# Step sizes ahead of z in the scan layer's front part, a second bank for its first projections, and fewer state slices summed by TensorE

## What is computed

```
x = _layernorm(x + _L0_attn_ref(x, ...))        # scan layer
x = _layernorm(x + _L0_xattn_ref(x, ctx_768, ...))
x = _layernorm(x + _L0_ffn_ref(x, ...))         # 4 experts, 2 of them used
x = _layernorm(x + _L1_attn_ref(x, ...))        # attention, 16 heads
x = _layernorm(x + _L1_xattn_ref(x, ctx_768, ...))
x = _layernorm(x + _L1_ffn_ref(x, ...))         # recurrence over the batches

def _L0_attn_ref(x, ...):
    xn = layernorm(x) * ln_g + ln_b
    xh, z = jnp.split(xn @ W_in, 2, axis=-1)
    conv = conv_b + sum over k of conv_w[:, k] * (xh shifted by 3 - k)
    xc = silu(conv)
    xpj = xc @ W_xp                              # B (16), C (16), one step size
    dt = softplus(xpj[..., -1:] @ W_dt + b_dt)
    h[t] = exp(dt * A) * h[t-1] + dt * B * xc    # for each of 16 states
    y = sum over states of h * C + xc * D
    return y * silu(z) @ W_out + x
```

## Time and profile before

| | |
|---|---|
| median of 3 runs | 1427.11 us (1426.35 to 1427.77) |
| the profiled execution, device time | 1427.31 us |
| its span in the trace | 1425.5 us |
| TensorE busy | 1221.3 us (86% of the span) |
| VectorE busy | 1112.3 us (78%) |
| ScalarE busy | 785.0 us (55%) |
| mean granted TensorE clock | 0.93 |

### The profile page before, as it was taken

One profiled execution on the slowest core, in us unless ns is written; L12 is line 12 of the kernel. 1 busy time (PEld: TensorE's weight loads), 2 busy tenths in 40 slices (PEclk: granted clock), 3 DMA queues, 4 the chain that ended last, 5 costly groups with the idle time before them and its releaser, 6 DMA issues.

```text
span 1425.5 us, 16890 instructions
## 1 busy us (share of the span) xinstructions
PE 1221.3 (86%) x6016; PEld 973.1 (68%) x6016; DVE 1112.3 (78%) x1799; ACT 785.0 (55%) x1861; POOL 122.4 (9%) x151
## 2 busy tenths in 40 slices
PE   3587778989989899989999899999998998999862
PEld 2454556677767767776777677877786767868742
DVE  2799699799978988899989997899889883343116
ACT  1533445385465663766667666675576645545521
POOL 0000111010011002110110010101000100010001
PEclk8788889999999999999999999999999999999976
DMA  4610111200011002010111001100210000000301
GB/s 165 218 72 4 71 38 30 67 30 31 11 65 56 31 1 75 8 49 30 46 37 49 31 29 54 49 30 1 75 49 19 12 15 20 1 0 8 117 0 59
DMA packets 27638, 62.53 MB, mean 44 GB/s; under 512 B 2346, under 2 KB 13451, under 8 KB 26915
## 3 DMA queue, kind: packets, MB, share of 16 engines
q1 hardware_dynamic: 27554, 61.46, 12.6%
HBM read 55.42 MB, written 6.04 MB: 43 GB/s over the span
## 4 chain that ended last, share of the span: by engine, by line
DVE 43%; PE 36%; issue 9%; ACT 9%; POOL 2%; DMA 0%; DVEq 0%; SPq 0%; ACTq 0%; POOLq 0%
DVE scans L496 12%; PE bank L283 12%; DVE scans L492 7%; PE bank L1065 4%; PE bank L447 4%; DVE scans L502 4%; PE bank L1083 3%; DVE nmax L1219 3%; DVE conv L383 2%; PE bank L851 2%; PE bank L633 2%; ACT scans L470 2%; PE bank L1110 2%; PE bank L845 2%; DVE scans L500 2%
## 5 line engine op out<-in xcount | busy, mean ns | idle before, releaser
L496 DVE TENSOR_TENSOR_SCAN scans<-scans 128x1024 f32<-128x1024 f32 x128 | 292.7, 2287 | 11.2 <-ACT scans L470 9.4
L470 ACT ACTIVATE scans<-dt,a_neg 128x255 f32<-128x255 f32 x512 | 222.4, 503 | 113.3 <-DVE scans L496 112.9
L447 PE MATMUL bank<-scans,ident 128*128 128x256 f32 x704 | 201.1, 425 | 21.5 <-DVE scans L500 15.4
L447 PEld LDWEIGHTS bank<-scans,ident 128*128 128x128 f32 x704 | 143.4, 214 | 57.8 <-DVE scans L500 25.0
L492 DVE TENSOR_TENSOR scans<-conv,BC 128x1024 f32<-128x1024 f32 x128 | 155.6, 1216 | 14.3 <-PE bank L447 13.9
L1153 ACT ACTIVATE ya<-bank,nmax 128x256 f32<-128x256 f32 x256 | 107.1, 472 | 96.1 <-DVE nmax L1219 95.9
L1219 DVE TENSOR_REDUCE nmax<-bank 128x2 f32<-128x512 f32 x128 | 87.2, 682 | 67.4 <-PE bank L1065 67.0
L1083 PE MATMUL bank<-v,ya 128*128 128x65 f32 x1024 | 133.9, 276 | 6.1 <-ACT yo L1144 6.1
L1083 PEld LDWEIGHTS bank<-v,ya 128*128 128x128 f32 x1024 | 131.2, 199 | 10.4 <-issue 6.7
L502 DVE TENSOR_TENSOR scans<-scans,BC 128x1024 f32<-128x1024 f32 x80 | 97.5, 1219 | 1.0
L283 PE MATMUL bank<-xnT,w_in 128*128 128x256 f32 x256 | 73.9, 440 | 20.8 <-DVE conv L383 12.8
(11 more groups left out here) (255 smaller groups left out, 2170.9 us busy)
## 6 DMA issues: line engine op xcount, KB each, us to landing
BC<-xpj_scratch SPq DMA_DIRECT2D x32, 1024.0 KB, 5.5
xin<-in_x SPq DMA_DIRECT2D x8, 256.0 KB, 2.8
conv<-in_x SPq DMA_DIRECT2D x8, 256.0 KB, 2.8
out<-scans SPq DMA_DIRECT2D x8, 256.0 KB, 2.6
kept_x<-x SPq DMA_DIRECT2D x7, 256.0 KB, 2.0
kept_w<-wa SPq DMA_DIRECT2D x7, 256.0 KB, 2.0
BC<-kept_w SPq DMA_DIRECT2D x1, 1792.0 KB, 8.5
scans<-kept_x SPq DMA_DIRECT2D x1, 1792.0 KB, 13.2
```

Source lines behind the costliest of these rows:

```text
L447: last = pe.matmul(sums_of(c), ident[:, :], hb[u % 2][:, i, :], start=False, stop=(h == UH - 1 and i == summed(b) - 1), skip_group_check=True)
L470: ins = act.activation(dA[u % 2][:, j, 1:S], dt[b % 2][:, c, 1:S], ACT.Exp, scale=a_neg[:, c, n:n + 1])
L496: dve.tensor_tensor_scan(flat(H[:, :, :]), flat(dA[u % 2][:, :, :]), flat(H[:, :, :]), 0.0, ALU.mult, ALU.add).then_inc(s["a_scan"], 1)
```

## The change

- **Order in the front part.** The projections j = 2 and 3, their tanh and their product (z) stand behind dt on TensorE, ScalarE and VectorE, and no longer between the convolution and xc. The turn of the next batch waits for z in place of dt.
- **Two banks in batch 0.** Projection j = 1 of batch 0 goes to bank 2 (SA[1], not yet in use), so it doesn't wait for the convolution of j = 0.
- **The place of xpj.** It lies in rows of xin, no longer of xnT, because xnT is still needed for z. So x of the next batch is loaded only when the store has landed and the step size has been spread (`a_store`, `a_dtl_ps`); ScalarE's xnT no longer waits for the store.
- **Sums.** FULL_SUMS becomes SUMMED = (4, 4, 4, 2, 2, 1, 1, 1): in batches 5, 6 and 7 VectorE adds the two remaining slices as well (a new `tensor_tensor` of 256 columns, behind a wait on its own result), and TensorE adds one.
- **Waits at the start.** `skips`, wt0, kzE and kzO are VectorE pieces of W now (two pieces, both still first in its order); TensorE waits for each where it uses it.
- **All order strings are new.** 1100 letters of TensorE, 1018 of ScalarE, 885 of VectorE (883 before), 74 of GpSimd and 91 of SyncE.

```diff
-FULL_SUMS = 3
+SUMMED = (4, 4, 4, 2, 2, 1, 1, 1)
...
     "sp": (
-        "FWFFSSWWWSWWSFFSSSSFFSSSSSSFFSSSWSWWWSSFFSSWWWWSSFFSSSWWWWSSFFSSSWWWWSSFSSWSWWWSSWSWWWWWWWW"
+        "FWFSSWWWFSWWSFFSSSSFFSSSSSSFFSSSWSWWWSFFSSSWSWWWFFSSSSFFWSWWWSSSSWWWWSFSWSSSWWWSSWSWWWWWWWW"
...
-        xpj = xnT[0:2 * NS + 1, 0, :]
+        xpj = xin[0:2 * NS + 1, 0, :]
...
         def front_sp(sp, b):
             if b:
-                sp.wait_ge(*of("a_xnT_ps", b - 1))
+                sp.wait_ge(*of("a_store", b - 1))
+                sp.wait_ge(*of("a_dtl_ps", b - 1))
...
+        def conv_bank(b, j):
+            return SA[1] if b == 0 and j == 1 else f0
...
             if b:
-                pe.wait_ge(*of("a_dt", b - 1))
+                pe.wait_ge(*of("a_silu_z", b - 1))
             turn(pe, xin, f0).then_inc(s["a_xnT_ps"], 1)
...
-            for j in range(4):
-                if 1 <= j <= 2:
-                    pe.wait_ge(*of("a_conv", b, 2 * j))
-                elif j == 3:
-                    pe.wait_ge(*of("a_silu_z", b, 1))
...
+            for j in range(2):
+                if j and b:
+                    pe.wait_ge(*of("a_conv", b, 2 * j))
+                projected(j, conv_bank(b, j))
                 yield
             pe.wait_ge(*of("a_xc", b))
-            pe.wait_ge(*of("a_silu_z", b))
             mm(pe, f0[0:2 * NS + 1, 0:S], [(w_xp[:, c, :], xc[:, c, :]) for c in range(EC)]).then_inc(s["a_xpj_ps"], 1)
...
+            pe.wait_ge(*of("a_dt", b))
+            for j in range(2, 4):
+                if j == 3:
+                    pe.wait_ge(*of("a_silu_z", b, 1))
+                projected(j, f0)
+                yield
...
         def summed(b):
-            return HN if b < FULL_SUMS else HN // 2
+            return SUMMED[b]
...
-                    dve.tensor_tensor(flat(H[:, 0:HN // 2, :]), flat(H[:, 0:HN // 2, :]), flat(H[:, HN // 2:HN, :]), ALU.add).then_inc(s["a_hC"], 1)
+                    last = dve.tensor_tensor(flat(H[:, 0:2, :]), flat(H[:, 0:2, :]), flat(H[:, 2:4, :]), ALU.add)
+                    if summed(b) == 1:
+                        own.link(last)
+                        last = dve.tensor_tensor(H[:, 0, :], H[:, 0, :], H[:, 1, :], ALU.add)
+                    last.then_inc(s["a_hC"], 1)
...
-            pe.wait_ge(s["prep_zero"], 3 + EC)
```

More of the change, by code:

```diff
@@ L304, in front_sp @@
             yield
+        SA = bank[1:3]
+        def conv_bank(b, j):
+            return SA[1] if b == 0 and j == 1 else f0
         def front_pe(pe, b):
@@ L371, in front_act @@
             yield
+            for j in range(2):
+                act.wait_ge(*of("a_in_ps", b, j + 3))
+                act.activation(flat(zg[b % 2][:, 2 * j:2 * j + 2, :]), f0[:, :], ACT.Tanh).then_inc(s["a_z_tanh"], 1)
+                yield
         def front_dve(dve, own, b):
@@ L405, in front_dve @@
             yield
+            for j in range(2):
+                z = flat(zg[b % 2][:, 2 * j:2 * j + 2, :])
+                dve.wait_ge(*of("a_z_tanh", b, j + 1))
+                dve.scalar_tensor_tensor(z, z, 1.0, f0[:, :], ALU.add, ALU.mult).then_inc(s["a_silu_z"], 1)
+                yield
         def front_pool(pool, own, b):
@@ L410, in front_pool @@
             yield
-        SA = bank[1:3]
         def sums_of(c):
@@ L1054, in y_pe @@
             yield
+            if b == 0:
+                pe.wait_ge(s["prep_zero"], 3)
             pe.wait_ge(*of("t_kz", b))
@@ L1313, in halves, with zeros @@
             dve.wait_ge(s["prep_halves"], 3)
+        def zeros(dve):
+            for c in range(EC):
+                dve.tensor_scalar(skips[:, c, :], ident[:, :], d_skip[:, c:c + 1], None, ALU.mult).then_inc(s["prep_skips"], 1)
+            dve.memset(wt0[CTX2:P, 1, :], 0.0).then_inc(s["prep_zero"], 1)
+            yield
+            dve.memset(kzE[HD:P, :, :], 0.0).then_inc(s["prep_zero"], 1)
+            dve.memset(kzO[0:HD, :, :], 0.0).then_inc(s["prep_zero"], 1)
+            yield
         def p_dve(dve, own):
+            yield from zeros(dve)
             dve.wait_ge(s["prep_pe"], 1)
```

87 lines of the change are left out of this document (38 added, 49 removed).

## The result

The changed kernel takes **1444.62 us** (median of 4 runs, 1442.38 to 1445.34) beside 1426.76 us for the kernel before in the same series: a ratio of 1.0119, 95% interval 1.0106 to 1.0132. It is 17 us slower by that ratio (18.0 in the profiled spans, 1443.5 beside 1425.5). The prediction was 1417 us, faster, with a range of 1398 to 1431: wrong in sign and outside its range.

A forecast was written before the change was run, and what follows sets the result against it. No engine alone bounds the kernel: VectorE early, both nearly full in batches 5 to 7, TensorE at the end. Terms -10.0 + 2.5 - 1.1 - 6.3 + 9.5 - 5.0 = -10.4 us: 1417 us, range 1398 to 1431.

The forecast's parts named there:

- The head: Front part of batch 0: a shorter chain starts the first unit at 46.0 instead of 56.04 us, gain 10.0 us.
- The bound of 7 us: Lower bound of the head's gain (bounds 7 and 13), expected if the skill's clock rule alone held.
- Batch 0's scan: First stage: +2.5 us of VectorE work, -1.1 us of waiting for dt; batch 0's residual 8.6 us earlier.
- Batches 1 to 4: Pieces put off, weighed by chain shares: 6.3 us earlier by batch 4's end; ends 9.7 and none.
- Batches 5 to 7: Additions and returning put-off pieces, weighed by chain shares: 9.5 us later; ends 26.6 later and 5.3 earlier.
- VectorE's idle time stays: Outer end for batches 5 to 7: VectorE's idle time does not fall, so 26.6 us come in.
- Behind the last scan: After batch 7's scan: fewer Y and W pieces left on TensorE, 5 us earlier.
- VectorE decides in batches 5 to 7: Rival: additions between scan and sum, VectorE's idle time unchanged, 26.6 us come in: 1434 us, chance 0.12.
- TensorE decides: Rival: from 154 us on, time follows TensorE's work, -27.7 us in all: 1399 us, chance 0.17.
- The clock: Rival: TensorE's clock falls by 0.02 over 425 us of work, costing some 8 us: 1425; 0.15 with the lost start.
- the 0.96 that I had named as a sign: Stages of batches 5 to 7: a clock under 0.96 was to show the forecast wrong.
- The early start lost: Rival: the first stage ends no earlier than before, 8.6 us go: 1425 us; chance 0.15 together with the clock.

The follow-up runs named there:

- e15: Changed kernel without the 48 additions of batches 5 to 7, TensorE still summing one slice a unit there: 1428.32 us, ratio 1.0012 to the kernel before.
- e6: Changed order up to batch 0's first units, z behind dt in batch 0 only, then the old order, no additions: 1425.56 us, 0.9994 of the kernel before.
- e12: e6 with TensorE's sum of the first unit moved ahead of the transposition of batch 1's x: 1421.85 us, ratio 0.9966 to the kernel before.
- e3: Changed kernel up to the end of batch 4's scan, then the old order, two slices, no additions: 1423.8 us, ratio 0.9991 to the kernel before.
- e14: Kernel before, TensorE summing one slice a unit in batches 5 to 7, no additions on VectorE: 1422.08 us, ratio 0.9969 to the kernel before.
- e2: Kernel before with only the changed sums (additions on VectorE, one slice on TensorE in batches 5 to 7): 1440.04 us, ratio 1.0098.
- e1: Changed kernel without the additions of batches 5 to 7, TensorE summing two slices, new order throughout: 1443.94 us, ratio 1.0124 to the kernel before.
- e4: Changed kernel up to the end of batch 4's scan, then the old order, with the additions: 1441.56 us, ratio 1.011 to the kernel before.
- e9: Changed kernel, TensorE summing only 16 of 256 columns of the remaining slice in batches 5 to 7: 1444.19 us, ratio 1.0122 to the kernel before.
- e13: Changed kernel with the additions kept, but TensorE summing two slices a unit in batches 5 to 7: 1447.24 us, ratio 1.0142 to the kernel before.

## Why the prediction was wrong

**The head: right.** Predicted 46.0 for the first unit, measured 45.80 (44.0 to 45.8 in the twelve profiles that begin with this order); xpj was ready at 35.8 (35.3). The bound of 7 us, which I had drawn from the Trainium skill's rule (page "TensorE: Matmul & The Clock Gate", section "HAM oscillation — how this bites in real kernels": bursts with idle gaps between run throttled), was not reached: skips and w_xp both ran slow, which cost 1 us more than I took, but the 16 preparation matmuls ran fast again, in 3.72 us.

**Batch 0's scan: mis-sized.** I counted +1.4 us; the stage is 8.5 longer (7 to 8.5 in eleven of the twelve profiles that begin with this order, 14 in e15). VectorE's work there is 3.7 us more, not 2.5. The rest is idle time, 13.1 us beside 8.3: 3.7 us of waits for the foldings and 1.1 for a convolution, in a stage whose idle time before was nearly all at its end. The folding's matmuls ran slow (the group of 512 columns 842 ns each, 626 before). e6 and e12 show such a wait ahead of a strictly ordered queue at work: one sum behind one transposition cost 5.8 us, and moving it brought the residual 3.8 us forward. The changed kernel has the sum ahead of the transposition, so there the waits are others; none of them was tested alone, and how much of them is the order and how much the slow matmuls is open.

**Batches 1 to 4: right place, wrong meaning.** The residual of batch 4 was predicted near 709 and came at 708.4, with a larger gain in these four stages (13.7 instead of 6.3) making up for batch 0. But I had priced a put-off piece as a gain where it is put off, by chain share, and its return as a cost by chain share. Both went at more than the length of either engine's work: the four stages were 13.7 us shorter with 11.0 us less on TensorE and 7.1 less on VectorE, and e3's next stage was 15.1 longer with 11.8 and 7.2 more.

**Batches 5 to 7: the step that failed.** Forecast +9.5, ends -5.3 and +26.6, measured +44. I had VectorE's work right (437 us predicted, 440.5 measured) and wrote that it fits only if its idle time falls from 48 to 21 us. It rose to 61. TensorE I had at 420 us, and it was 440.6. Three terms were wrong. First, weighing a relief of TensorE and a load on VectorE by the shares of the chain, 0.36 and 0.43: in the old order they are worth 0.2 and 0.9 of their length (e14, e2; 4.4 and 18.4 us). Second, taking it that an order of pieces costs nothing beyond its work: this one costs 20 us where there is no addition (e1 against e3), though only 3 beside the additions. Third, counting TensorE's records at one length: taken form by form at their mean durations in the kernel before, those of the three stages took some 21 us more in the changed kernel and 8 more in e1, none in e3 (5 of the 21 are sums that now come one at a time, 329 ns of busy time each instead of 278). The outer end, "VectorE's idle time stays", was thought a worst case and was not.

By the runs, the way from 1425.5 to 1443.5 us is: -15.4 at batch 4's residual; +13.2 because put-off pieces come back (e3: 714.9 us from there, before 701.7); +20.1 by the new order of batches 5 to 7 and the end (e1: 735.0); +0.1 for the additions against the records in that order (735.1), which is +3.7 in the stages and -3.6 at the end by its clock. Sum +18.0. The split of the last two depends on the way taken: over e4 (731.9 us) it is +17.0 for the additions and +3.2 for the order. Only their sum, 20 us, belongs to the change; each hides the other.

**Behind the last scan: -10.6 instead of -5.** Some of it is clock. e1 and e9 have the same pieces there and took 236.9 us at 0.88, the clock of the kernel before in its 244.0 us; the changed kernel had 0.90. So 7 us are the pieces' and 3.6 the clock's.

**The rivals.** *VectorE decides in batches 5 to 7*, with 0.12, had the right side and 26.6 of 44 us. *TensorE decides* is refuted for the old order: 21.8 us of its work were worth 4.4. *The clock*: the three stages ran at 0.96, 0.93 and 0.94 instead of 1.00, 0.98 and 0.97, two of them below the 0.96 that I had named as a sign. e1 has 0.98, 0.96 and 0.94 and the same time, so the depth of the fall did not set the time, and e1's slower records are 8 us of TensorE's time beside a loss of 20. Whether idle time lowered the clock or the clock made idle time, no run separates. *The early start lost*: by the residual of batch 0 four fifths of it were (1.7 us ahead instead of 8.6), and the forecast of batch 4 came out right only because batches 1 to 4 gained 7 us more than I had counted: that number was luck. Two slips changed nothing: the chances for "faster" add up to 0.75, not 0.76, and TensorE was 93 to 94% busy in three stages, not four (92% in batch 7's).

## What to carry to other kernels

Don't price a relief on one engine and a load on another by their shares of the chain that ended last. Where two engines are over 90% busy, test each alone and both together (leave the work out on one, then add it on the other): here one was worth 0.2 and the other 0.9, and in another order each hid the other. The same holds for two causes of a loss: from batch 4 on, taking away the additions alone gained nothing and the order alone 3 us, both together 20. A lead in the middle of a program counts only if the pieces done by then are the same; count the pieces that were put off, and take them at their full length on both engines, not at a share of it. And in a strictly ordered queue look first at the one cheap instruction that others wait for (a sum that frees a buffer), and at what stands ahead of it.

## What the runs showed of the hardware

**A narrow matmul is not cheap.** Records of 128x16 took 178 to 375 ns, 241 on average, where those of 128x256 took 413: a sixteenth of the columns for more than half of the time. By busy time the 96 records fell from 31.6 to 15.8 us. The 128x128 float32 weight load ahead of each stayed as it was, 199 ns beside 204.

**GpSimd was held up by VectorE.** The power over 2 columns took 0.70 us at 1011.05 and 2.60 us at 1005.08, when it met a scan: it ended 0.5 us behind the scan's end. The Trainium skill says on its page "SBUF — State Buffer", section "Who interferes with whom", that a VectorE instruction with two SBUF inputs contends with a GpSimd instruction that reads SBUF, for a pair of ports that one of them locks, and that the order of issue decides which is blocked. The trace agrees: the scan had started 0.17 us ahead of the power, and the power ended behind it (scan's end 1004.91 + 2.28 = 1007.19, power's end 1007.68).

**The same code under another clock.** Batch 0's stage, with the same pieces, took 105.4 us at a clock of 0.79 (e13) and 112.1 us at 0.73 (e15), while the stages of batches 1 to 4 took 126.1, 127.1, 154.1 and 148.5 us in each of the runs that keep the new order that far, to 0.1 us. Differences of a few us between two profiles in the first stage or behind the last scan say nothing about the code.
